# Two graph layers with a state-space scan: new block order, earlier first chain, staged stores, and two products moved from GpSimd to VectorE

## What is computed

```python
# layer 0, a graph convolution and a Mamba block over the 4096 rows
h = relu(adj @ x @ gcn_w + gcn_b);  h = layernorm(h) * ln_g + ln_b
xc, z = split(h @ w_in);  u = silu(causal_conv4(xc));  dbc = u @ w_xp
dt = softplus(dbc[:, :8] @ w_dt + b_dt)                 # 256 channels
hst = exp(dt*A) * hst + dt * B * u;   y = hst @ C       # scan, 16 states per channel
y = (y + u * D_skip) * silu(z)
x1 = layernorm(x + y @ w_out)
# layer 1
out1 = mlp3(2 * (adj @ x1), W1);   out2 = mlp3(2 * (adj @ x2), W2)
out  = layernorm(x1 + concat(out1, out2) @ Wm.T + bm)
```

## Time and profile before

| | us |
|---|---|
| median of 3 runs | 832.26 (831.99 to 838.22) |
| the profiled execution's own time | 836.52 |
| its span, first to last instruction | 834.7 |
| PE busy | 808.9 (97%) |
| GpSimd busy | 662.5 (79%) |
| VectorE busy | 606.0 (73%) |
| ScalarE busy | 380.1 (46%) |
| HBM read | 223.43 MB |

### The profile page before, as it was taken

How to read it: one execution, slowest core, us unless ns; L and a number is a source line. 1 busy time by engine, 2 the same in 40 slices (tenths; PEclk the granted TensorE clock), 3 DMA queues, 4 the chain that set the end, 5 groups by cost and what they waited for, 6 DMA issues and landing times.

```text
span 834.7 us, 7328 instructions
## 1 busy us (share of the span) xinstructions
PE 808.9 (97%) x2074; PEld 366.1 (44%) x2074; DVE 606.0 (73%) x805; ACT 380.1 (46%) x615; POOL 662.5 (79%) x322
## 2 busy tenths in 40 slices
PE   6999989999999999999999999999989999999995
PEld 2444434444444444444444444444434444444453
DVE  0020998789878978997799889888987897752134
ACT  0043575347534753575357535753565362301234
POOL 2002999999999999999999999999988999800046
PEclk9999998999999999999999999999999999999998
DMA  8978865865766788767886778799999999968602
GB/s 342 397 295 278 268 211 190 297 210 197 266 249 192 245 284 297 260 245 235 272 286 222 245 266 298 236 367 357 355 326 335 340 355 383 397 254 278 225 25 77
DMA packets 63101, 226.56 MB, mean 271 GB/s; under 512 B 7362, under 2 KB 8276, under 8 KB 44628
## 3 DMA queue, kind: packets, MB, share of 16 engines
q1 hardware_dynamic: 24084, 155.28, 50.2%
q10 hardware_dynamic: 38976, 70.80, 26.6%
HBM read 223.43 MB, written 2.62 MB: 271 GB/s over the span
## 4 chain that ended last, share of the span: by engine, by line
PE 88%; DVE 5%; DMA 2%; POOL 1%; issue 1%; ACT 1%; ACTq 1%; POOLq 0%; DVEq 0%
PE p_x L484 48%; PE p_x L505 18%; PE p_two L505 8%; DVE p_h L907 3%; PE p_m L576 2%; PE p_m L592 2%; DVE prod L916 1%; PE p_dA L663 1%; DMA x_s<-x_tiles 1%; POOL mb L410 1%; PE p_two L566 1%; PE p_m L596 1%; PE p_m L588 1%; PE p_m L530 1%; PE p_m L559 1%
## 5 line engine op out<-in xcount | busy, mean ns | idle before, releaser
L484 PE MATMUL p_x<-ring,x_s 128*128 128x512 f32 x1024 | 459.9, 600 | 7.8 <-DMA x_s<-x_tiles 7.8
L1097 POOL TENSOR_TENSOR y<-y,prod 128x1024 f32<-128x1024 f32 x127 | 298.8, 2353 | 18.4 <-DVE prod L916 17.6
L484 PEld LDWEIGHTS p_x<-ring,x_s 128*128 128x128 f32 x1024 | 195.2, 192 | 259.6 <-issue 249.1
L1088 POOL TENSOR_TENSOR bh<-spread,dtu 128x1024 f32<-128x1024 f32 x128 | 301.5, 2356 | 1.8 <-DMA spread<-bc_rows 1.8
L907 DVE TENSOR_TENSOR_SCAN p_h<-p_dA,state,bh 128x512 f32<-128x512 f32 x224 | 276.2, 1279 | 32.1 <-ACT p_dA L673 17.9
L673 ACT ACTIVATE p_dA<-dt,A 128x512 f32<-128x512 f32 x256 | 171.8, 687 | 148.6 <-DVE p_h L907 141.8
L505 PE MATMUL p_x<-ring,x 128*128 128x512 f32 x352 | 158.0, 598 | 0.8 <-issue 0.8
L916 DVE TENSOR_TENSOR prod<-p_h,spread_C 128x1024 f32<-128x1024 f32 x128 | 155.4, 1214 | 0.2 <-issue 0.2
L505 PEld LDWEIGHTS p_x<-ring,x 128*128 128x128 f32 x352 | 66.3, 191 | 84.0 <-issue 84.0
L410 POOL TENSOR_SCALAR mb<-prod,mv,rstd 128x128 f32<-128x128 f32 x30 | 23.4, 793 | 76.9 <-ACT rstd L894 76.2
L932 DVE TENSOR_TENSOR acc<-p_x,acc 128x512 f32<-128x512 f32 x30 | 20.7, 689 | 72.9 <-PE p_x L505 72.9
(11 more groups left out here) (122 smaller groups left out, 578.5 us busy)
## 6 DMA issues: line engine op xcount, KB each, us to landing
ring<-adj_blocks SPq DMA_DIRECT2D x143, 1024.0 KB, 7.0
spread<-bc_rows ACTq DMA_DIRECT2D x128, 256.0 KB, 4.8
spread_C<-bc_rows ACTq DMA_DIRECT2D x128, 256.0 KB, 5.6
x_s<-x_tiles SPq DMA_DIRECT2D x8, 256.0 KB, 7.3
x_s<-x_tiles ACTq DMA_DIRECT2D x7, 256.0 KB, 17.0
out_tiles<-mb SPq DMA_DIRECT2D x7, 256.0 KB, 2.0
pack<-pack_w ACTq DMA_DIRECT2D x1, 1026.5 KB, 23.9
ring<-adj_blocks SPq DMA_DIRECT2D x4, 256.0 KB, 4.3
```

Of the source, the lines that this page charges most:

```text
L484: last = pe.matmul(bank[:, :], tiles[:, j, :], ring[:, i % RING, jt, :], start=j == 0, stop=j == N // P - 1)
L1088: pool.tensor_tensor(bh[:, i % 3, :, :], both(spread[:, i % SLOTS, :]), dtu[:, c % 2, :, :], ALU.mult).then_inc(s_bmul, 1)
L1097: pool.tensor_tensor(y[:, c % 2, :, :], y[:, c % 2, :, :], prod[:, i % 2, :, :], ALU.add).then_inc(s_acc, 1)
```

## The change

- **Blocks.** A block is now (parts, row group, column group), and x2 and x1 can share a load (`DOUBLE`). The order is written out for each chunk (`CHUNK_BLOCKS`), there are 145 blocks where there were 144, and the partial sums are listed (`SUMS`, 30 as before). The matmuls for blocks in chunks 0 to 7 are 80, 80, 84, 80, 80, 88, 84, 76, where each chunk had 80, and 5 blocks of 4 matmuls follow chunk 7 ahead of the tail, where 8 did.
- **First chain.** `FILL` has 14 matmuls ahead of dt and 18 behind it (29 and 3 before), the four bias products (L609) stand behind gcn, the first two broadcasts of B are issued ahead of the softplus, and `take_x(1)` stands in unit 0 of chunk 0.
- **Spacing.** dt stands half a unit later in chunks 1 to 6, the steps of the MLP on x2 a unit apart (half a unit before), and `origin(0)` is 4.
- **Start.** Three matmuls on zeros run ahead of the data; the first x tiles come in two transfers, not four.
- **End.** Four staging buffers (in `dtu`, free by then) replace the two of `mb`, and VectorE normalises group 6 and half of group 7, not only the latter.
- **GpSimd to VectorE.** `dtu` and `gate_y` are made by VectorE.

```diff
-FILL = {"gcn": 3, "cen": 3, "var": 5, "in_x": 13, "x_proj": 5, "dt": 3}
+FILL = {"gcn": 0, "cen": 1, "var": 3, "in_x": 7, "x_proj": 3, "dt": 18}
@@ origin, mlps, chain_steps
-    return 3 if c == 0 else 4
+    return 4
-        return [(c - 1, (24, 25, 26, 27))]
-    return [(6, (6, 8, 10, 12)), (7, (26, 27, 28, 29))]
+        return [(c - 1, (24, 26, 28, 30))]
+    return [(6, (6, 8, 10, 12)), (7, (24, 26, 28, 30))]
-        at = (6, 8, 10, 12, 16, 18) if c == 0 else tuple(2 * origin(c) + q for q in (-1, 1, 2, 4, 9, 11))
+        at = tuple(2 * origin(c) + q - (c == 0) for q in (-1, 1, 2, 4, 9, 12))
@@ normalise
-            if k >= 2:
-                eng.wait_ge(s_out[k % 2], 16 * (k // 2))
+            if k >= STAGES:
+                eng.wait_ge(s_out[k % STAGES], 16 * (k // STAGES))
@@ block.tensor
+            pe.wait_ge(s_idle, 1)
+            for _ in range(WARM):
+                pe.matmul(p_m[:, 0:WARM_W], sq[:, 0:P], sq[:, 0:WARM_W], start=True, stop=True)
@@ block.scalar
-                if name == "softplus":
-                    take_x(1)
+                if name == "rows":
+                    for i in range(AHEAD):
+                        spread_row(i)
...
+                    if c == 0 and unit == 0:
+                        take_x(1)
@@ block.vector
+                elif name == "dtu":
+                    dve.wait_ge(s_dt, G * (n + 1))
+                    dve.wait_ge(s_u, G * (n + 1))
+                    dve.tensor_tensor(dtu[:, b, :, :], dt_[:, b, :, :], u[:, :, :], ALU.mult).then_inc(s_dtu, 1)
+                elif name == "gate_y":
+                    dve.wait_ge(s_acc, S * (n + 1))
+                    dve.wait_ge(s_gate, n + 1)
+                    dve.tensor_tensor(y[:, b, :, :], y[:, b, :, :], gate[:, :, :], ALU.mult).then_inc(s_yg, 1)
...
                 if c:
+                    put(0, 1, "gate_y", c - 1)
                     put(3, 0, "out", c - 1)
...
                     put(o + 7, 0, "dt_sum", c + 1)
+                    put(o + 7, 0, "dtu", c + 1)
...
-            normalise(dve, NC - 1, range(JT // 2, JT), NC, s_fin_last)
+            normalise(dve, NC - 2, range(JT), NC - 2, s_fin_dve)
+            normalise(dve, NC - 1, range(JT // 2, JT), NC, s_fin_dve)
@@ block.gpsimd
-                    if unit == 0 and c:
-                        step("gate_y", c - 1)
-                    if c + 1 < NC and unit == origin(c) + 8:
-                        step("dtu", c + 1)
```

More of the change, by code:

```diff
@@ L45 @@
 PACK_W = _at
-HALVES = {"one": (0, 1), "x": (0,), "x2": (1,)}
-def block_steps(blk):
-    kind, n, k = blk
-    if kind == "two":
-        return [(0, jt) for jt in range(JT)]
-    halves = HALVES[kind][::-1] if (kind, n, k) == ("one", 2, 0) else HALVES[kind]
-    return [(half, jt) for half in halves for jt in range(JT)]
-RAMP = [("x", 0, k) for k in range(NBLK)]
-FILL_BLOCKS = [("x", 1, k) for k in range(NBLK)]
-FILL = {"gcn": 3, "cen": 3, "var": 5, "in_x": 13, "x_proj": 5, "dt": 3}
-_ones = [("one", n, k) for n in range(2, NC) for k in range(NBLK)]
@@ L95, with row, mixed @@
-AFTER_BLOCKS = [("two", 6, k) for k in range(NBLK)]
-AFTER = len(AFTER_BLOCKS)
-TAIL_BLOCKS = [("two", NC - 1, k) for k in range(NBLK)]
+def row(what, n, columns):
+    return [(what, n, m) for m in columns]
+ALL = range(NBLK)
+ONE, X, X2, X1, DOUBLE = ("x", "x2"), ("x",), ("x2",), ("x1",), ("x2", "x1")
+def mixed(*lists):
+    return [b for q in range(max(len(p) for p in lists)) for p in lists for b in p[q:q + 1]]
+RAMP = row(X, 0, ALL)
+FILL_BLOCKS = row(X, 1, ALL)
+FILL = {"gcn": 0, "cen": 1, "var": 3, "in_x": 7, "x_proj": 3, "dt": 18}
@@ L99 @@
+AFTER_BLOCKS = row(X1, 0, (6,)) + row(X1, 1, (6,)) + row(X1, 6, (6,)) + row(X1, 5, (5, 6))
+TAIL_BLOCKS = [b for n in range(NC) for b in row(X1, n, (NC - 1,))]
+X2_ROWS = (2, 3, 4, 0, 1, 5, 6, 7)
+X1_FIRST = (0, 1, 5, 6)
+SUMS = [("two", 2, (0, 1)), ("two", 3, (0, 1)),
+        ("two", 4, (0, 1)), ("two", 0, (0, 1, 2)),
+        ("two", 1, (0, 1)), ("two", 1, (2, 3)),
[4 rows of a table added]
+SUMS += [(("x2", "x")[n % 2], n, (NC - 1,)) for n in range(NC)]
+BANK = [bank for bank, _, _ in SUMS]
 LOADS = RAMP + FILL_BLOCKS
@@ L100 @@
 FIRST = []
-for _c in range(NC):
+for _blocks in CHUNK_BLOCKS:
     FIRST.append(len(LOADS))
-    LOADS = LOADS + chunk_blocks(_c)
+    LOADS = LOADS + _blocks
 AFTER_AT = len(LOADS)
@@ L463, in _, with first @@
+            for q in range(STAGES):
+                sp_.wait_ge(s_out[q], 16 * (NC // STAGES + (q == k % STAGES)))
         @block.tensor
         def _(pe):
-            def one(i, lo, hi):
-                kind, n, k = LOADS[i]
+            def first(i, part, jt):
+                _, n, m = LOADS[i]
+                bank, tiles, s_taken, taken = ((p_x, x_s, s_ax, n) if part == "x" else
+                                               (p_x2, x2_s, s_ax2, X2_ROWS.index(n)))
+                opens = jt == 0 and i == FIRST_OF[part, n]
+                closes = jt == JT - 1 and i == LAST_OF[part, n]
+                if opens:
+                    wait(pe, s_taken, taken)
+                if part == "x2" and jt == 0 and i < FIRST[1]:
+                    pe.wait_ge(s_x2s[m], 16)
+                return pe.matmul(bank[:, :], tiles[:, JT * m + jt, :], ring[:, i % RING, jt, :],
+                                 start=opens, stop=closes)
@@ L488, in one @@
[L488 to L508 removed]
+                for q in range(lo, hi):
+                    part, jt = steps[q]
+                    last = second(i, jt, chunk, unit) if part == "x1" else first(i, part, jt)
+                    if q == len(steps) - 1:
+                        last.then_inc(s_blk_used, 1)
+                    elif part == "x" and jt == JT - 1 and i == LAST_OF[part, LOADS[i][1]]:
+                        last.then_inc(s_px, 1)
@@ L617, in _ @@
                 if name == "gcn":
+                    for q in range(2 * G):
+                        last = pe.matmul(p_h[:, 1, q:q + 1], w_in[:, P * q:P * (q + 1)], w("ln_b"),
+                                         start=True, stop=True)
+                    last.then_inc(s_bxzp, 1)
                     pe.wait_ge(s_cen_w, 1)
@@ L1024, in _ @@
             dve.wait_ge(s_two_add, 1)
-            for name in ("var", "taps0", "taps1", "x_sum", "dt_sum"):
+            for name in ("var", "taps0", "taps1", "x_sum", "dt_sum", "dtu"):
                 step(name, 0)
```

297 lines of the change are left out of this document (127 added, 170 removed), and 4 rows, old and new, of the table SUMS.

## The result

The changed kernel takes **823.31 us** in the median (822.81 to 823.63), the kernel before 832.4 us beside it (831.99 to 838.22): a ratio of 0.9873, 95% interval 0.9836 to 0.991, so 1.3% faster (0.9 to 1.6). At the medians the gain is 9.1 us; the sum of the prediction said 12.8. So 823.31 lies within the range (814.5 to 829) and 1.3 us above the forecast of 817 to 822. The profiled executions differ by more: 834.7 us of span before, 821.3 after, 13.4 us.

What follows compares the result with a forecast made beforehand. PE was taken as the bound, losing time to waits, the low clock behind them and the ends. Terms -8.7 -4.1 -0.9 +1.3 +0.6 -1.0 +0 = -12.8 us take the 832.26 us median to 819.5; range 814.5 to 829.

Steps and rivals of the forecast that it cites:

- z to z of chunk 0: Time between z starts on PE in chunk 0: 85.85 us falls to 77.1 with earlier scans, -8.7 us.
- -4.1 us of chunk 6: Chunk 6 on PE: dt half a unit later removes its 2.3 us wait and the clock loss behind it.
- The price of the first chain, +1.3: Ahead of chunk 0: fewer fillers before dt make PE wait for step inputs, +1.3 us.
- the upper one, being nearest to that row: dtu and gate_y on VectorE: bounds 1.22 and 3.6 us each; 3.6 taken, as if blocked by a GpSimd instruction.
- +0.6 us for small leftovers: Moving dtu and gate_y to VectorE: delays mostly hidden behind existing waits, +0.6 us booked.
- my walk through chunk 4: Units 0 to 2 of chunk 4: unit 1's work ends 3.9 us later, at 413.7, before unit 2's 414.06: hidden.
- the give-back in small waits: Rival, 15%: late hr or dbc costs PE 1.9 us in each of 7 chunks, 13 us back, about 832.
- VectorE becomes the bound: Rival, 7%: each moved product waits for two GpSimd instructions, 88 us per chunk against 82.4, about 859 us.
- the difference is what I trust, not the level: Whole kernel: the -12.8 us of profiled span was subtracted from the 832.26 us median, though the profiled run took 836.52.
- -13.1: From z of chunk 0 to the tail on PE: forecast change, -8.7 -4.1 -0.9 +0.6 us.
- -0.9 us for the bank wait: Ahead of the last out: PE's 0.83 us wait for an addition in the same bank goes, -0.9 us.
- the start and the end: Ramp: warm-up taken as 0, bounds 0 and -1.7 us. Tail: normalising split between VectorE and GpSimd, -1.0 us.

Runs made afterwards that it cites:

- three versions on the way: Products moved to VectorE on the kernel before (840.14 us), on it with the first chain (835.27), and with first chain and dt half a unit later (832.9).
- second profile of before: The kernel before, unchanged, profiled once more: 834.62 us measured, ratio 1.0006, span 832.1 us.

## Why the prediction was right, and where it was not

**Right: the mechanism, with luck in the sum.** PE's waits with the clock behind them were the loss, chunk 0 from scans that began late and chunk 6 from a dt without room. z to z of chunk 0 was forecast as 77.1 and is 77.14; the first scan "near 70" is at 70.83; no wait ahead of dt is left, and the clock is 1.00 from 18 us on. The first chain and the spacing alone bring 10.3 of the 11.5 us that separate the changed kernel with its products on GpSimd from the kernel before in the same comparison. The -4.1 us of chunk 6 appear by themselves with the edit of one number. The price of the first chain, +1.3, was 1.1. That the total agrees as well as it does is luck: the errors below have both signs.

**Mis-sized: the products, "the upper one, being nearest to that row".** 3.6 us each was taken, 1.2 to 1.3 is the median. The row that I used for it, an operation on 4 columns, was measured beside a GpSimd that was busy without a gap. In the changed kernel most products fall into gaps of GpSimd, which waits 55.9 us in all for VectorE's products with C. That is a matter of place, not of load: the kernel before with the products on VectorE has 47.8 us of such gaps, and there the median was 2.35 and 2.25 us. The two of 3.3 us started 0.1 us behind a GpSimd instruction of 2.37. The rule of the Trainium skill ("SBUF — State Buffer", section Who interferes with whom), that the later of the two is blocked for the whole of the other, gives 2.37 less the 0.1, and 1.22: 3.5 us, near to these. It fits the other way round as well: a GpSimd addition of 2.35 us that starts 0.2 us behind the gate takes 3.2. It was more than one instruction three times: 4.90, 4.95 and 7.96 us were measured, through two, two and three instructions of GpSimd. In 18 other gate products the next GpSimd instruction was queued just the same, and VectorE's came between; no row shows what decides.

**Right in size, but not for the reason given: "+0.6 us for small leftovers".** The move costs 0.3 us in the spans of the changed kernel (821.3 and 821.0). But my walk through chunk 4, where all was hidden, was made in the one place that was never in danger. The rival that came, in three versions on the way, is the first, the give-back in small waits: the move cost 5.7, 6.8 and 8.6 us there, and in the last two no product took over 3.4. The rival "VectorE becomes the bound", with two GpSimd instructions ahead of a product, was dismissed because the earlier trace rows never show more than one; that did happen, but to one product each in three versions, in chunk 0 and at its end, and never to all. What kept the give-back away is, by the runs, `origin(0)` with its move of var and in_x, lines of the change for which the prediction has no term; the changed kernel itself was not run without them.

**Failed: "the difference is what I trust, not the level".** 819.5 was made as 832.26 less a difference of spans, and the profile had taken 836.5. Of its 4.3 us above the median 1.05 us of chunk 0 went into the sum, and the ramp's 1.7 us of clock into the 13.4 between the spans. Against the second profile of before (832.1) the change of span is 10.8 us, and 834.5 less 823.0 in the medians of that comparison is 11.5. An execution that is above the median by the very losses that the change removes makes the gain too large. Why the kernel before takes 832.4 in the first comparison and 834.2 to 834.6 in the others is open, and with it whether the gain is 9.1 or 11.5.

**Failed: no new waits.** Of the MLP steps the prediction said that they "only change places", and of the blocks only that they remove a wait. Three waits came that the sum has no term for ("a new wait for a bank's addition" stands among the prediction's own signs of being wrong, and the third is near to that): 1.76 us ahead of the second MLP step of group 6 in chunk 7, 0.78 for a row's bank, 0.53 for a sum in the bank from which VectorE still takes dt: 3.07 us, nearly the whole difference between -13.1 and -10.0 in the table. The first is not due to a step that moved: those of group 6 stand where they stood. Taking PE's waits away in chunk 6, and blocks out of chunk 7, brought PE to a step for which ScalarE had been in time by only 0.7 us. I did not look at what ScalarE has in its order just ahead of that activation; half a unit later the wait is gone.

**Mis-sized: the blocks.** -0.9 us for the bank wait is right by itself, it is gone; but the new blocks bring new bank waits of 1.3 us (the 0.78 and 0.53 above). Nothing is left.

**Mis-sized: the start and the end.** The clock of the ramp came back, 1.7 us, where I took 0 with that as the bound; it came back without the warm-up too. The end brought 2.8 us where I took 1.0: I let VectorE and GpSimd exclude each other as in the earlier trace rows, and their rows show no such thing; both took their time side by side. Yet the earlier trace rows do show one: of its eight instructions the seven beside a GpSimd product end 0.02 to 0.04 us behind such a product, the one without takes 0.17. Both VectorE operations are TENSOR_SCALAR with one tensor input; GpSimd made a product in the one case and a TENSOR_SCALAR in the other. Which of the differences matters no run here separates.

## What to carry to other kernels

Where engines run fixed programs, moving the start of one earlier can be undone at the next point at which its order ties it to the late one: here a copy for which ScalarE waited 6.7 us. Look for such a wait behind the edit. Taking one engine's waits away brings it to steps that others had ready just in time: list the margins of the steps behind, not only the waits. Whether an operation could move to another engine was not decided in the middle chunk, where all is hidden, but at both ends. Count from the last wait at the start, not from zero, when two profiles are compared. And read two profiles of the kernel before: what only one of them shows does not belong into the sum.
